# Selective scans of a Mamba block: the softplus sum as an accumulating DMA, and five in place of four products with B on GpSimd

## The reference, cut to what matters

```
dt = softplus(einsum('brl,dr->bdl', dt, dt_w) + dt_b[None, :, None])     # d = 512 channels
A = -exp(A_log)                                                          # 16 states a channel
def step(h, inp):
    dt_t, B_t, C_t, u_t = inp
    h = exp(dt_t[..., None] * A) * h + (dt_t * u_t)[..., None] * B_t[:, None, :]
    return (h, einsum('bdn,bn->bd', h, C_t))
```

## Time and profile before

| | |
|---|---|
| median of 3 runs | 9198.21 us (9195.44 to 9199.81) |
| the profiled execution | 9194.41 us, its span 9192.7 us |
| forward scans / reverse scans | about 2860 to 4640 us / 4675 to 6480 us of the span |
| busy over the span | PE 91%, DVE 83%, ACT 53%, POOL 39% |
| TensorE's mean granted clock | 0.958 |
| DMA over the span | 615.81 MB, 67 GB/s |

### The profile page before, as it was taken

The page is one execution under the profiler, slowest core; times in us unless marked ns, Lnnn a source line. Parts: engine busy times, 40 slices in busy tenths (PEclk is TensorE's granted clock), DMA queues, the critical chain, the costliest instruction groups (busy, mean ns, idle before and its releaser), DMA issues. The chain is left out here.

```text
span 9192.7 us, 130248 instructions
## 1 busy us (share of the span) xinstructions
PE 8340.8 (91%) x35938; PEld 3452.2 (38%) x35938; DVE 7658.0 (83%) x10977; ACT 4879.4 (53%) x7770; POOL 3581.8 (39%) x1746
## 2 busy tenths in 40 slices
PE   7999999999998888888878888888679999999999
PEld 3333333345543333333333333333533333333455
DVE  7888888876666999999979999999278888888666
ACT  3566666642234666665655555555026666666421
POOL 0001000000005999999969999999000000000000
PEclk8899999999999999999989999999879999999999
DMA  6111211122152222222223222222660211111221
GB/s 173 24 25 26 34 25 25 25 51 64 53 192 92 73 68 67 69 66 68 67 88 94 85 87 84 84 87 85 198 156 17 32 26 25 25 25 25 60 64 46
DMA packets 569122, 615.81 MB, mean 67 GB/s; under 512 B 204225, under 2 KB 374209, under 8 KB 568481
## 3 DMA queue, kind: packets, MB, share of 16 engines
q1 hardware_dynamic: 568480, 608.05, 24.7%
HBM read 434.15 MB, written 172.15 MB: 66 GB/s over the span
## 5 line engine op out<-in xcount | busy, mean ns | idle before, releaser
L740 DVE TENSOR_REDUCE ffn_att_mx<-psum 128x1 f32<-128x512 f32 (+3 forms) x4708 | 2909.1, 668 | 541.8 <-PE psum L573 298.7
L697 ACT ACTIVATE ffn_att_e<-psum 128x1024 f32<-128x1024 f32 (+3 forms) x2560 | 2180.8, 895 | 1161.3 <-PE psum L633 1155.7
L570 PE MATMUL psum<-ffn_att_k,ffn_att_q 96*128 96x512 bf16 (+3 forms) x5388 | 1845.1, 361 | 81.0 <-DMA ffn_att_v<-v 76.7
L537 POOL TENSOR_SCALAR_AFFINE_SELECT ffn_att_e<-ffn_att_e 128x512 f32<-128x512 f32 x512 | 324.8, 634 | 3234.6 <-ACT ffn_att_e L697 3234.6
L633 PE MATMUL psum<-ffn_att_q,ffn_att_k 99*128 99x512 bf16 (+3 forms) x5120 | 1500.4, 349 | 27.2 <-issue 26.3
L1517 POOL TENSOR_TENSOR scan_r_h<-scan_r_h,scan_r_cs 128x1024 f32<-128x1024 f32 x512 | 1195.3, 2357 | 202.4 <-ACT scan_r_state L1678 199.1
L1517 POOL TENSOR_TENSOR scan_f_h<-scan_f_h,scan_f_cs 128x1024 f32<-128x1024 f32 x512 | 1193.7, 2357 | 178.9 <-ACT scan_f_state L1678 175.8
L600 PE MATMUL psum<-ffn_att_e,ffn_att_v 128*32 128x512 f32 (+3 forms) x10240 | 1204.0, 542 | 5.1 <-ACT ffn_att_o L716 4.3
L1596 PE MATMUL psum<-scan_f_h,ident 128*128 128x512 f32 x2048 | 1035.0, 647 | 138.6 <-POOL scan_f_h L1517 138.4
L1596 PE MATMUL psum<-scan_r_h,ident 128*128 128x512 f32 x2048 | 997.1, 629 | 126.8 <-POOL scan_r_h L1517 126.0
L570 PEld LDWEIGHTS psum<-ffn_att_k,ffn_att_q 96*128 96x128 bf16 x5388 | 522.0, 98 | 1419.0 <-DVE ffn_att_mx L740 991.1
(11 more groups left out here) (211 smaller groups left out, 8673.6 us busy)
## 6 DMA issues: line engine op xcount, KB each, us to landing
scan_f_cs<-scan_f_bcd SPq DMA_DIRECT2D x264, 256.0 KB, 3.4
scan_r_cs<-scan_r_bcd SPq DMA_DIRECT2D x264, 256.0 KB, 3.4
ffn_att_q<-q_parts SPq DMA_DIRECT2D x72, 384.0 KB, 6.4
q_parts<-ffn_in_q SPq DMA_DIRECT2D x192, 128.0 KB
scan_f_win<-xp SPq DMA_DIRECT2D x18, 1036.0 KB, 7.2
scan_r_win<-xp SPq DMA_DIRECT2D x18, 1036.0 KB, 7.2
ffn_att_q<-q_parts SPq DMA_DIRECT2D x72, 256.0 KB, 8.0
mamba_out_ys<-yz SPq DMA_DIRECT2D x18, 1024.0 KB, 7.0
```

Of the source, the lines that this page charges most:

```text
L570: ins = nc.tensor.matmul(at, q[0:PARTS, i // HALF, h, i % HALF * P:(i % HALF + 1) * P], k[0:PARTS, c * P:c * P + w], start=True, stop=not ...
L697: nc.scalar.activation(E[:, s % PB, 2 * hp:2 * hp + 2, off:CH], psum[:, 2 * hp:2 * hp + 2, off:CH], ACT.Exp, scale=HD ** -0.5).then_inc(e_ ...
L740: nc.vector.reduce_max(mx[:, heads[0]:heads[-1] + 1, i // HALF, i % HALF, c // TT], psum[:, turn, 0:len(heads) * w].rearrange("p (h w) -> ...
```

## The change

Three things. The tuple `POOL_N` has five states (3, 6, 9, 12, 15) in place of four (3, 7, 11, 15), so that DVE makes 11 of the 16 products of a chunk and GpSimd 5. GpSimd's `softplus` no longer adds: it waits for the logarithms and issues a DMA from `sp1` to `dt[par]` that adds onto the target, and counts `dt_added` up by 16 when it has landed. `times_u` on GpSimd and two waits on ScalarE (the first decay of a chunk, the first softplus input of a chunk, which overwrites `sp1`) wait for `dt_added` in place of `dt_ready`; the first chunk's own sum on DVE still counts `dt_ready`.

```diff
-    POOL_N = (3, 7, 11, 15)
+    POOL_N = (3, 6, 9, 12, 15)
...
                 def softplus(i, par):
-                    pool.wait_ge(logs, DM * (i + 1))
-                    nc.gpsimd.tensor_tensor(dt[par][:, :, :], sp1[:, :, :], dt[par][:, :, :], ALU.add).then_inc(dt_ready, 1)
+                    hold(pool, logs, DM * (i + 1), pool_passed)
+                    nc.gpsimd.dma_start(dt[par][:, :, :], sp1[:, :, :], accum_op=ALU.add).then_inc(dt_added, 16)
 
                 def times_u(i, par):
-                    pool.wait_ge(dt_ready, i + 1)
+                    pool.wait_ge(dt_added, 16 * i)
                     pool.wait_ge(u_ready, i + 1)
...
                 def softplus_in(i, par, m, bank=BANK_X):
                     act.wait_ge(dt_ps, DM * i + m + 1)
-                    if m == 0:
-                        act.wait_ge(dt_ready, i)
+                    if m == 0 and isinstance(i, int) and i == 1:
+                        act.wait_ge(dt_ready, 1)
+                    elif m == 0 and not (isinstance(i, int) and i == 0):
+                        act.wait_ge(dt_added, 16 * (i - 1))
...
-                        if k == 0:
-                            act.wait_ge(dt_ready, i + 1)
+                        if k == 0 and first:
+                            act.wait_ge(dt_ready, 1)
+                        elif k == 0:
+                            act.wait_ge(dt_added, 16 * i)
```

More of the change, by code:

```diff
@@ L1382, in mamba_scan @@
         bcd = [nc.dram_tensor(f"{tag}_bcd{p}", (BC, CH), F32, kind="Internal").ap() for p in range(2)]
-        sp_passed = sem("sp_passed")
+        sp_passed, pool_passed = sem("sp_passed"), sem("pool_passed")
         cw_in, w_in, made, a_exp, a_neg, diags = (sem(n) for n in ("cw_in", "w_in", "made", "a_exp", "a_neg", "diags"))
@@ L1388, in mamba_scan @@
         dt_ps, dt_read, logs, dt_ready, du_ready = sem("dt_ps"), sem("dt_read"), sem("logs"), sem("dt_ready"), sem("du_ready")
-        exps = sem("exps")
+        exps, dt_added = sem("exps"), sem("dt_added")
         b_ps, decay = sem("b_ps"), sem("decay")
```

## The result

| | before | with the change |
|---|---|---|
| median | 9198.53 us (9195.44 to 9199.81, 4 runs) | 9093.96 us (9084.89 to 9098.28, 4 runs) |
| ratio | 1 | 0.9887, 95% interval 0.9875 to 0.9900 |
| span of the profiled execution | 9192.7 us | 9096.6 us |
| both scans | 3675.1 us | 3583.0 us |
| the rest of the span | 5517.6 us | 5513.6 us |

The change saves 104.6 us by the medians. "Both scans" is counted here from the first instruction of the forward call on VectorE (the memset of `scan_f_sel`) to the first result of `mamba_out`. The lines of the kernel have moved by a few: the scans are L1812, DVE's products L1778, the decays L1720, the state's copy L1680.

The account below looks back on a forecast made before the run. DVE's own instructions were taken to bound each scan chunk; 32 x 2.38 = 76.2 us off 9194.4, all else hidden or at nothing, gave 9118.2, or 9122 us against the median, range 9100 to 9225.

Parts of the forecast that it names:

- What bounds: In both scan stages DVE's own instructions set a chunk's pace; GpSimd follows with some 8 us of room.
- What DVE saves: One product with B less on DVE in each of 32 chunks, 2.38 us each: 76.2 us at most.
- What GpSimd gives and takes: On GpSimd the softplus sum (4.53 us) goes and a product (4.52 us) comes: 0.0 us in sum.
- The issue: GpSimd's issue of the adding DMA takes 1 us, covered by the 1.97 us that GpSimd is ahead.
- The lead: GpSimd ends the product for n=15 1.97 us earlier than before; the issue and DMA may use that up free.
- The landing: The DMA lands 8.4 us after issue (ends 5.5 and 12.4); up to 11.2 us costs nothing, 13.6 eats the gain.
- The late landing: Rival: slow DMA adder delays du and DVE in step 15; landing at 17 us gives 9307 us; chance 0.20.
- the partly late one: Rival: landing between 11.2 and 13.6 us, time between 9122 and 9198, 9160 at 12.4 us; chance 0.13.
- the sum: Total of the terms: 9194.4 - 76.2 = 9118.2 us, or 9122 against the median.
- more than the product: Rival: unused GpSimd lead removes part of DVE's 15.5 us forward waits for TensorE's row of B; down to 9102 us.
- What else moves: SyncE's fifth row of B a chunk stays hidden; buffer reuse builds no lag; ScalarE's new waits come tens of microseconds later.
- The dear issue: Rival: the issue holds GpSimd as long as the sum it replaces, 4.53 us; 9204 us, no change; chance 0.07.

Follow-up runs that it names:

- dma_alone: Kernel before with only the softplus sum as an adding DMA, GpSimd keeping its four products: 9187.81 us, ratio 0.9991.
- early_both: Changed kernel with the last convolution half in step 13, its copy in step 14, and TensorE's sum of step 13 behind step 15's row of B: 9072.98 us.
- add_step10: Changed kernel with the adding DMA issued in step 10 in place of step 9, du still in step 11: 9197.96 us, ratio 1.0002.
- add_step11: Changed kernel with the adding DMA issued in step 11, right ahead of du: 9348.52 us, ratio 1.0168.
- late_early: early_both with the adding DMA issued one step later, in step 10: 9134.31 us, ratio 0.9931.
- four_dmas: Changed kernel with the sum as four adding DMAs of 256 KB in place of one of 1024 KB: 9142.01 us, ratio 0.9942.
- plain_copy: Changed kernel with GpSimd's DMA as a plain copy, the addition left out: 9091.65 us (one run).

## Why the prediction was wrong, point by point

**What bounds.** DVE's own instructions take most of a chunk, as said. But "GpSimd follows with some 8 us of room" was wrong in the place that matters: the 8.4 us of waits lie in other steps than 9 to 15, where GpSimd's extra work is; its timeline shows 2.36 of them ahead of step 8 and none behind it.

**What DVE saves.** 2.38 us was forecast and 2.43 measured, 77.8 in place of 76.2. The mean of 11.83 and 11.93 took in the second pair of steps, which has a wait of its own; the first pair alone gives 2.43.

**What GpSimd gives and takes.** Right: the DMA was to be issued 3807.05 - 3792.87 = 14.18 us after DVE's product of step 9, and is, at 3789.41 - 3775.26 = 14.15.

**The issue.** 1 us was taken, 0.60 measured by the starts. The lead that is left is 1.97 - 0.60 = 1.4 us, and the starts show it: from DVE's product of step 9 to du it is 3818.26 - 3792.87 = 25.39 before and 24.00 with the change.

**The landing.** 8.4 us was taken, 7.0 measured, 8.7 at most, below the 11.2 from which it was to cost. By the runs it costs from the 9.85 at which du starts. The late landing and the partly late one fell; the reason given for 8.4, two source reads between SBUF and SBUF, had the right direction (7.0 against 4.7 for a copy).

**The step that failed is the sum.** It took 76.2 us for the product off the profiled time and put everything else at nothing: DVE's waits in the scans, and the 5518 us outside them, since the two scan stages were "the only ones that the change touches". For the stages outside no reason was given beyond that, and no rival either. Measured, the product gives 77.8, the wait for the row of B 11.9, and some 10 us go outside the scans.

The wait was named, in the rival "more than the product", as part of 15.5 us, and its reason was right; 11.9 of the 15.5 went, nearly all that can (dma_alone leaves 3.1, early_both 3.5). But that rival was priced down to 9102, 20 us below the sum, which is more than the whole row. So the wait alone doesn't lead out of the range: with 77.8 + 11.9 the sum would have been 9194.4 - 89.7 = 9104.7, and 9108.5 against the median. From there to 9094.0 are 14.5 us: about 10 outside the scans, 2.4 more in the scans (92.1 - 89.7), and some 2 left over, which is less than the two medians of the changed kernel differ by (3.3).

Of the signs named, du without idle time, a landing below 11.2 and an issue near 1 us came true; the chunk was to be 106.5 and 108.2 us and is 105.7 and 108.2, so the reverse stage is as forecast and the forward one has the waits in addition.

**The same mistake with the other sign.** "The lead that the issue and the DMA may use up before anything is later than now" doesn't exist: 1.6 us of added issues cost 1.65 a chunk, and 3.1 us of late landing cost the whole gain of 92 us and 11 more. That each microsecond is lost beyond the threshold was about right, but the threshold was wrong. The chain is not only GpSimd's product for n=15: the moves of early_both, which change only the order of the sums, the last convolution half and its copy, take 47 of 103 us of the cost away. Through what the rest goes is argued from the waits, not tested.

**The 10 us outside the scans** put the time out of the range: without them the median would lie inside, near 9104. They arise in code that the change doesn't touch, no row of before pointed to them, and their cause is open.

**What else moves.** The fifth row of B on SyncE costs nothing: its loads land in 3.4 us, those of C in 3.2 (3.4 before). No wait for them shows.

**The dear issue** fell with 0.60 us.

## What to carry to other kernels

When work leaves an engine that another in-order engine waits for, look at everything that stands behind that wait in the second engine's queue, not at the one consumer that was named: here a good part of GpSimd's lateness, 47 of 103 us, went through what stood behind its sums on TensorE, and a slack counted at one consumer was no slack. Test a two-part change by its parts: a DMA that frees 4.5 us of GpSimd, and a product that takes 2.4 off VectorE, were worth 8 and -1 us of the scans alone and 92 together; by the waits, each alone relieved one engine and left the other in the way. And an accumulating DMA is a good place for an elementwise sum whose result isn't needed for two steps; how far from its reader it is issued decides whether it is (add_step10 lost all of the gain by one step). And a forecast that leaves the untouched stages out takes a measurement for them as given; here they moved by 10 us of 9200.

## What the runs showed of the hardware

- An adding DMA of 1 MB from SBUF to SBUF lands in 7.0 us, a copying one in 4.7. Issued a step or two later, with the same size, it took 8.5 (8.4 at least in add_step10, add_step11 and late_early); which work beside it makes the difference wasn't tried. Quarters of it, issued together, took 5.2 each (median).
- GpSimd is held for 0.60 us by an issue (the four of four_dmas hold it for 2.22 together), though the trace gives the instruction 0.59 for the copy and 0.86 for the addition. In the stretch behind it its instructions read longer, du 4.79 in place of 4.54 us, while the starts keep their pace: from du to h times C of step 12 it is 3803.75 - 3799.26 = 4.49, before 3822.76 - 3818.26 = 4.50. Where GpSimd waited for the landing, in add_step11, du read 4.49, and behind the copying DMA of plain_copy 4.52. So the pace is to be taken from starts here.
- TensorE loses 16.9 to 17.5 us to "issue" ahead of L633 of the second attention with four products on GpSimd and 8.1 to 9.5 with five, though the code of that stage is the same; no cause was found.
- Behind a wait of 3.61 us TensorE's eight matmuls took 5.40 us, at a mean granted clock of 0.78, where without such a wait two times four take 1.98 each (add_step10 and the change).
